# Half of the key tiles of a cross attention turned by VectorE and four transfers a head instead of by TensorE

## The reference

```python
x = layernorm(x + self_attention(x))                 # one head, masked, D = 512
q, k, v = (Q @ Wq + bq), (K @ Wk + bk), (V @ Wv + bv)   # Q = x, K = V = ctx, 16 heads of 64
att = softmax(einsum('bhqd,bhkd->bhqk', q * scale, k))
out = einsum('bhqk,bhkd->bhqd', att, v)
x = layernorm(x + out @ Wo + bo)
x = layernorm(x + shared(x) + expert(x) + bias)
```

## Time and profile before

| | us |
|---|---|
| median of 3 runs | 1958.29 |
| lowest, highest | 1957.91, 1958.37 |
| the profiled execution | 1957.6 |
| its span | 1955.7 |

### The profile page before, as it was taken

How to read it: one execution, slowest core, us unless ns; L and a number is a source line. 1 busy time by engine, 2 the same in 40 slices (tenths; PEclk the granted TensorE clock), 3 DMA queues, 4 the chain that set the end, 5 groups by cost and what they waited for, 6 DMA issues and landing times.

```text
span 1955.7 us, 29661 instructions
## 1 busy us (share of the span) xinstructions
PE 1943.1 (99%) x9863; PEld 1633.1 (84%) x9863; DVE 1475.4 (75%) x3136; ACT 1147.9 (59%) x2461; POOL 727.5 (37%) x858
## 2 busy tenths in 40 slices
PE   9999999999999999999999999999999999999998
PEld 8888888788888888888888888888888888788887
DVE  6766666787777777777777777777777788867887
ACT  5445554676666666666766666666666667732221
POOL 2222342233343433332433333233333343527763
PEclk9999999999999999999999999999999999999999
DMA  5777778863545636354553726355352537321221
GB/s 216 287 282 287 290 280 317 278 223 107 184 167 184 194 108 205 97 184 152 181 170 91 235 74 215 108 161 168 119 186 73 195 121 214 128 87 46 85 87 65
DMA packets 112086, 334.87 MB, mean 171 GB/s; under 512 B 9152, under 2 KB 9152, under 8 KB 107200
## 3 DMA queue, kind: packets, MB, share of 16 engines
q1 hardware_dynamic: 111792, 332.72, 51.0%
q10 hardware_dynamic: 144, 0.26, 0.0%
HBM read 211.31 MB, written 88.08 MB: 153 GB/s over the span
## 4 chain that ended last, share of the span: by engine, by line
PE 95%; DVE 2%; ACT 2%; issue 1%; POOL 0%; ACTq 0%; DVEq 0%; POOLq 0%
PE a_proj L1334 17%; PE a_turned L1334 17%; PE a_score L1347 11%; PE a_av L1371 11%; PE a_proj L48 9%; PE a_proj L1358 5%; PE a_turned L1358 5%; PE a_proj L1762 4%; PE a_av L1762 4%; PE a_score L48 3%; PE a_av L48 3%; ACT c_prob L1042 1%; PE a_score L1737 1%; PE a_turned L1721 1%; PE a_turned L623 1%
## 5 line engine op out<-in xcount | busy, mean ns | idle before, releaser
L981 POOL TENSOR_SCALAR c_prob<-c_prob,all_rden 128x512 f32<-128x512 f32 x512 | 348.6, 693 | 883.5 <-DVE all_rden L1151 883.5
L1042 ACT ACTIVATE c_prob<-a_score,all_negmax 128x512 f32<-128x512 f32 x512 | 347.6, 684 | 212.0 <-DVE all_negmax L1145 209.2
L1145 DVE TENSOR_REDUCE all_negmax<-a_score 128x1 f32<-128x512 f32 x512 | 329.4, 685 | 186.8 <-PE a_score L1347 186.4
L1347 PE MATMUL a_score<-c_ks,c_qs 128*128 128x512 f32 x1024 | 277.6, 391 | 3.2 <-ACT c_prob L1042 2.9
L1371 PE MATMUL a_av<-c_pt,c_vs 128*128 128x512 f32 x1024 | 277.1, 391 | 0.0
L1347 PEld LDWEIGHTS a_score<-c_ks,c_qs 128*128 128x128 f32 x1024 | 190.5, 188 | 44.7 <-ACT c_prob L1042 5.9
L1371 PEld LDWEIGHTS a_av<-c_pt,c_vs 128*128 128x128 f32 x1024 | 192.0, 188 | 39.8
L1191 DVE TENSOR_TENSOR c_pt<-a_proj,c_pt 128x512 fp32r<-128x512 f32 x258 | 171.9, 686 | 26.9 <-ACT c_pt L1070 24.9
L1334 PE MATMUL a_proj<-all_second_buffer,c_wq 128*128 128x512 f32 x756 | 188.0, 397 | 0.0
L1334 PE MATMUL a_turned<-all_third_buffer,all_first_buffer 128*128 128x512 f32 x732 | 182.6, 398 | 0.0
L1191 DVE TENSOR_TENSOR c_pt<-a_turned,c_pt 128x512 fp32r<-128x512 f32 x254 | 169.0, 686 | 9.0 <-ACT c_pt L1070 5.3
(11 more groups left out here) (215 smaller groups left out, 3278.0 us busy)
## 6 DMA issues: line engine op xcount, KB each, us to landing
all_first_buffer<-ctxT_scratch SPq DMA_DIRECT2D x64, 512.0 KB, 7.7
c_wk<-wk_scratch SPq DMA_DIRECT2D x64, 512.0 KB, 3.9
c_wq<-wq_scratch SPq DMA_DIRECT2D x64, 512.0 KB, 6.0
all_second_buffer<-x1T_scratch SPq DMA_DIRECT2D x16, 2048.0 KB, 14.7
c_ks<-c_ks SPq DMA_DIRECT2D x128, 256.0 KB, 6.9
ctxT_scratch<-s_csp SPq DMA_DIRECT2D x8, 2048.0 KB, 7.4
c_y<-y_steps_scratch SPq DMA_DIRECT2D x16, 1024.0 KB, 6.3
y_steps_scratch<-c_y SPq DMA_DIRECT2D x15, 1024.0 KB, 10.2
```

Of the source, the lines that this page charges most:

```text
L981: nc.gpsimd.tensor_scalar(prob[:, n % 2, i, :], prob[:, n % 2, i, :], rden[:, n % 2, i:i + 1], 1.0, ALU.mult, ALU.mult).then_inc(p_ready, 1)
L1042: nc.scalar.activation(prob[:, n % 2, i, :], spsum[:, i % 2, :], ACT.Exp, bias=negmax[:, n % 2, i:i + 1], scale=1.0, accum_out=den[:, n % ...
L1145: nc.vector.tensor_reduce(negmax[:, n % 2, i:i + 1], spsum[:, i % 2, :], AX.X, ALU.max, negate=True).then_inc(smax, 1)
L1347: ins = nc.tensor.matmul(spsum[:, i % 2, :], qs[:, j % 2, e, i * P:(i + 1) * P], ks[:, j % 2, e, m, :], start=(m == HI), stop=(m == LO))
```

## The change

**Two key tiles of four leave PE.** For all heads but the first two and the last (`WHOLE`), key tiles 2 and 3 are turned another way (`FLIPPED` = 2), key tiles 0 and 1 as before. One step turns one tile now (`turned_in`).

**The flip.** DVE transposes squares of 32x32 (`flip`): of each query tile the 256 keys of the two key tiles, 128x256 elements from `prob` to `squares_out`. It reads every fourth key, since a square holds the keys j*4+m of one m. The flips of a step's two tiles stand behind the two maxima of the next step.

**The transfers.** SP sends a head's squares to `landing` with four transfers of 128 KB (`send_squares`): each takes 32 partitions with 4 KB and writes 128 partitions with 1 KB. Two steps later ACT rounds the landed tile to its high part (`flip_hi_tile`) and POOL subtracts it for the low part, in place (`flip_lo_tile`). So two low parts of four move from DVE to POOL.

**The query order.** The columns of a turned tile are now in the order a, i, q (quarter of a query tile, tile, place). PE's transposes write their 128 columns in four pieces of 32, and `o_first` and `o_second` put them back in order. `o_first` writes to `osum` itself, which has room for two pairs, and the sum of a head follows two steps later than its last value.

**The order of projections** is changed in `MIDDLE`, `FIRST` and `LAST`. **The bulk loads** (operands of the next group, Wv, Wo) are issued by ACT in pieces, two behind each of the steps 3, 4 and 6 to 11 (`BULK`); x1T is loaded in four pieces. SP's program goes by steps. The feed-forward weights are stored in pieces, two of its buffers lie elsewhere, and the semaphores `passed` are one.

The core of the diff:

```diff
-    NEXT = ["V0+", "K0+", "Q0+", "V1+", "V2+", "K1+", "Q1+"]
-    MIDDLE = ["V3", "K2", "Q2", "O0", "O1", "O2", "K3", "Q3", "O3"] + NEXT
-    FIRST = ["V2", "V3", "K2", "", "Q2", "", "K3", "", "Q3"]
-    NEXT_TO_FIRST = NEXT
-    LAST = ["V3", "K2", "Q2", "", "O0", "", "K3", "", "Q3", "", "O1", "", "O2", "", "O3", ""]
+    NEXT = ["V0+", "K0+", "Q0+", "V1+", "K1+", "V2+"]
+    MIDDLE = ["Q1", "K2", "Q2", "V3", "O0", "O1", "K3", "Q3", "O2", "O3"] + NEXT
+    FIRST = ["V2", "K2", "Q2", "V3", "", "", "K3", "", "Q3", ""] + NEXT
+    LAST = ["Q1", "K2", "Q2", "V3", "", "O0", "K3", "Q3", "", "O1", "", "O2", "", "O3", "", ""]
...
+    WHOLE = (0, 1, HH * GROUPS - 1)
+    FLIPS = {head: n + 1 for n, head in enumerate(h for h in range(HH * GROUPS) if h not in WHOLE)}
+    LANDINGS = {head: sum(h % 2 == head % 2 for h in FLIPS if h <= head) for head in FLIPS}
+
+    def turned_in(g, step):
+
+        n, half = divmod(step, 2)
+        return [(g, T * n + k) for k in ((2 * half, 2 * half + 1) if HH * g + n in WHOLE else (half,))]
+
+    def valued_in(g, step):
+
+        n, half = divmod(step, 2)
+        tiles = [(n - 1, 1)] if half else [(n - 2, 2), (n - 2, 3), (n - 1, 0)]
+        return [x for x in (tile_of(g, *tile) for tile in tiles) if x]
...
     def head_done(g, step):
 
-        if step % 2 == 0:
-            return None
-        n = (step - 3) // 2
-        return (g, n) if n >= 0 else (g - 1, HH - 1) if g else None
+        n = step // 2 - 2
+        return None if step % 2 else (g, n) if n >= 0 else (g - 1, n + HH) if g else None
...
+    def send_squares(g, n):
+        head = HH * g + n
+        sp.wait_ge(flipped, T * FLIPS[head])
+        wait(sp, av_mm, T * (head - 1))
+        for a in range(SQUARES):
+            sp.dma_start(as_f32(landing[:, head % 2, a, :, :]).rearrange("p k n -> p (k n)"),
+                         squares_out[head % 2][a * Q:(a + 1) * Q].rearrange("p m k i q -> p (m k i q)")).then_inc(
+                             landed[head % 2], 16)
...
+    def flip_lo_tile(g, n, k):
+        head = HH * g + n
+        pool.wait_ge(flip_hi, FLIPPED * (FLIPS[head] - 1) + k + 1)
+        whole = landing[:, head % 2, :, k, :]
+        nc.gpsimd.tensor_tensor(whole, as_f32(whole), by_square(as_f32(flip_hi_part[:, k, :])),
+                                ALU.subtract).then_inc(flip_lo, 1)
...
+    BULK = {3: [("v", (0, 1))], 4: [("v", (2, 3))], 10: [("o", (0, 1))], 11: [("o", (2, 3))], 6: [("c", 0), ("c", 1)], 7: [("c", 2), ("c", 3)], 8: [("x", 0), ("x", 1)], 9: [("x", 2), ("x", 3)]}
...
+    def flip_hi_tile(g, n, k):
+        head = HH * g + n
+        act.wait_ge(landed[head % 2], 16 * SQUARES * LANDINGS[head])
+        wait(act, av_mm, T * (head - 1) + TURNED + k + 1)
+        nc.scalar.copy(by_square(flip_hi_part[:, k, :]), as_f32(landing[:, head % 2, :, k, :])).then_inc(flip_hi, 1)
...
+    def out_part(g, n):
+
+        return osum[sides(n % 2)[0], n // 2 % 2, :].rearrange("p (i a q) -> p i a q", i=T, a=SQUARES)
...
+                for operand, k in BULK.get(step, []):
+                    if operand in "cx":
+                        (load_ctx if operand == "c" else load_x)((g + 1) % NB, k)
+                    if operand == "v" and g % NB == NB - 1:
+                        load_half(act, WV, wvparts, g // NB + 1, wv_loaded, k)
+                    if operand == "o" and g % NB == 0:
+                        wait(act, wo_mm, T * g)
+                        load_half(act, WO, woparts, g // NB, wo_loaded, k)
...
+    def flip(g, t):
+        n, i = divmod(t, T)
+        head = HH * g + n
+        dve.wait_ge(p_ready, TILES * g + t + 1)
+        if i == 0:
+            wait(dve, landed[head % 2], 16 * SQUARES * (LANDINGS[head] - 1))
+        nc.vector.transpose(squares_out[head % 2][:, :, :, i, :].rearrange("p m k q -> p k m q"),
+                            prob[:, n % 2, i, TURNED * P:].rearrange("p (k j m) -> p k m j", k=FLIPPED, m=SQUARES)).then_inc(
+                                flipped, 1)
...
+            for tile in tiles:
+                max_tile(*tile)
+            for tile in ahead(g, step - 1):
+                if HH * tile[0] + tile[1] // T in FLIPS:
+                    flip(*tile)
+            if item and item[0] in "KQ":
+                for e in range(2):
+                    proj_lo_part(item, [e])
+                    if tiles:
+                        recip(*tiles[e])
             else:
-                if left:
-                    rest_of_hole(g, step - 1)
-                for tile in tiles:
-                    max_tile(*tile)
-                finish(item)
+                if item:
+                    finish(item)
                 for tile in tiles:
                     recip(*tile)
-                if head:
-                    o_second(*head)
-                pt_lo_tile(g, 2 * step)
-                pt_lo_tile(g, 2 * step + 1)
+            if head:
+                o_second(*head)
+            for tile in turned_in(g, step):
+                pt_lo_tile(*tile)
...
-            ins = nc.tensor.transpose(bank_of(("T", g, t))[:, i * P:(i + 1) * P],
-                                      prob[:, n % 2, i, k * P:(k + 1) * P], ident[:, :])
+                pe.wait_ge(p_ready, TILES * g + t + i + 1)
+            ins = nc.tensor.transpose(squares(bank_of(("T", g, t)))[:, i], prob[:, n % 2, i, k * P:(k + 1) * P],
+                                      ident[:, :])
...
+            for tile in valued_in(g, step):
+                values(*tile)
+            for tile in turned_in(g, step):
+                turn(*tile)
```

More of the change, by code:

```diff
@@ L1162, in proj_lo_part @@
         bias = bks if letter == "K" else bqs
-        for e in range(2):
+        for e in heads:
             rows, other = sides(e)
@@ L1427, in tensor_all @@
         me.after.gate(0, 0)
+        for t in range(TILES - FLIPPED, TILES):
+            values(GROUPS - 1, t)
         for item in EPILOGUE[:2]:
```

385 lines of the change are left out of this document (184 added, 201 removed).

## The result

The changed kernel takes 1884.54 us (median of 4 runs, 1883.14 to 1884.82), the kernel before 1958.15 us beside it (4 runs, 1957.91 to 1958.37). The ratio is 0.9623, 95% interval 0.9606 to 0.9639: 73.6 us less. The forecast was 1854, 30 us too low. The measured time lies inside the range of 1838 to 1925, but above the stretch of 1840 to 1874 that the forecast itself was given. The profiled execution took 1884.64 us, its span is 1882.7 us.

What follows compares the result with a forecast made beforehand. PE's instruction order was taken to bound the kernel between about 360 and 1730 us. Sum: 1957.6 - 109 (transposes) + 5 (late x1 operand) + 0.7 (end) = 1854 us; range 1838 to 1925, forecast stretch 1840 to 1874 at 0.60.

Steps and rivals of the forecast that it cites:

- rival 1: Cross attention: DVE takes over, its work equal to PE's step at 0.75 us a flip; 1874 to 1924 us, chance 0.11.
- rival 3: Landing of squares takes 15 us where queues are full, ACT stands 1 to 2 us; 1897 to 1945 us, chance 0.10.
- the signs of being right: Four transposes in 0.35 us, 5.00 us steps, PE at 100, flips near 0.42 us, no PE waits for landed low parts.
- the price of a transpose: PE, regular cross attention steps: eight transposes at 0.79 us become four at 0.35, 0.44 us less; 109 us in all.
- The step: PE's regular step in the cross attention falls from 5.44 us to 5.00 us.
- The flip: DVE, two a step: 0.42 us each for 128x256 elements, DVE's work 4.37 us a step, 87% of 5.00.
- The 0.68 us in the prediction: DVE's flip if reading every fourth float halved the rate: 0.68 us instead of 0.42, work 4.89 us a step, still hidden.
- rival 4: DVE's flip is three times as dear, 1.26 us, making the kernel slower at 2110 us; chance 0.07.
- The transfers: A head's squares land in 8 us, wanted by ACT after 11.4 us with some 2 us of slack.
- The operands: The next group's x1 operand may be late by 0 to 1.5 us, 15 times; 5 us taken.
- Rival 2: PE's remaining transposes slow from 110 to 188 ns writing four pieces of 32 columns; 82 us back, 1936 us, chance 0.06.
- The ends: First and last group: 12 steps without a projection lose one transpose chain of 0.35 us each, 4.2 us in all.

Runs made afterwards that it cites:

- The dense read: The changed kernel with the flip reading its keys side by side instead of every fourth, computing another attention: 1891.89 us (0.9661).
- other holes: The changed kernel with the last group's six steps without a projection moved to steps 5, 9, 11, 13, 14, 15: 1882.45 us (0.9618).

## Why the prediction was right, and what failed in it

**The range held by luck.** Its part above 1874 us was there for rival 1 (DVE takes over) and rival 3 (squares land late). Neither happened in the middle; the measured 1884.5 us came into it by a loss that no rival describes. Of the signs of being right, one failed: PE has rows that wait for low parts of landed tiles, 6.1 us in 12.

**The bound and the price of a transpose: right.** PE's order is the time in the middle, and four transposes are worth 0.426 us (forecast 0.44), shown by the period of the groups and once more by putting them back. The step is 5.01 us (5.00). Taking the price from starts of neighbouring chains, and not from the mean of 272 ns in the earlier trace rows, made this term. (The sum counts 12 changed steps without a projection. By the lists `FIRST` and `LAST` there are 10, two of them in the head that isn't flipped, so 8; that moves the sum by 0.4 us.)

**The flip: mis-sized, without effect in the middle.** 0.62 us instead of 0.42, and DVE at 91% instead of 87%. The dense read, at 0.42 us, shows that the whole difference is the stride of 16 bytes. The Trainium skill (SBUF — State Buffer, Door 1: The DMA port swizzle) says that each access that crosses to a new line of 16 bytes pays a penalty, and the trace agrees: the read costs 48% more, 622 ns against 419. The 0.68 us in the prediction was its own estimate, from a rate halved. Rival 1 would have needed a flip of about 0.8 us (estimated above from the run with more work on DVE), rival 4 by the forecast's own sum 0.96 us.

**The transfers: too dear.** 2.7 us at the median, 8.7 at most, so rival 3 fell. By the forecast's sum ACT wants them after 11.4 us. The operands cost 0.8 us of PE's waits in the middle, where 5 were allowed, and 3.4 us in all; 2.5 of these are for ctx, after which the prediction didn't ask. Rival 2 fell as well: a chain of four takes 0.36 us with its output in four pieces of 32 columns, against 0.35 in the earlier trace rows. The rule of the Trainium skill (same page and section) that any non-contiguous PSUM pattern slows matmuls doesn't show in this trace, for pieces of 32 columns.

**The ends: the step that failed.** The prediction gave 12 steps without a projection a gain of 0.35 us each, and 30 regular steps beside them 0.44, and asked after DVE, POOL and the score banks in regular steps alone. There a step has 5 us of PE's work over 4.6 us of DVE's. In a step without a projection PE has 1.7 or 2.6 us left (scores 0.91, values 0.46 or 1.37, a chain 0.35), and DVE still has two maxima, two flips, two reciprocals and a low part, 1.29 + 1.15 + 0.22 + 0.65 = 3.3 us, and in some an output sum besides. There PE need not be the bound, less work for it can be worth nothing, and each operation added elsewhere is a candidate for the path. The run with the transposes twice splits the 29 us: taking them out brought 10.3 of the 17.4 us at the ends, about what the 30 regular steps there would give at 0.426 (12.8), and the rest of the change cost 21.8 us there, which the forecast had at nothing. As time of PE, as far as trace and runs tell, the 29 us are:

- About 18 us are waits of PE. Its listed waits grew by some 19 us over the span (exponentials 2.9 to 9.4, low parts 6.1, ctx 2.5, the feed-forward's x2T 0.8 to 2.7, x1 0.9, two more of 1.0 and 0.4), of which 1.4 us fall into the middle. Of the loss at the start, 4 to 5 us come from heads 0 and 1 turned by PE in succession on single buffers; flipping head 1 shows it.
- Up to 7 us are the clock. In six windows of 10 us, all at the ends, the granted clock is 0.83 to 0.95; the sum of (1 - clock) x 10 us is 6.8 us, though not all of it is time in which PE had work. In the kernel before, the profiled execution had a mean clock of 1.00, here 0.996. It falls behind waits of PE (below). This is read from the trace; no run tried it alone.
- The rest, 4 us or more, is not placed. About 0.5 us of it stands ahead of the stage's first tiles: the same V projection starts at 347.30 us, before at 346.76.

The waits of the last group weren't shortened by other holes or by less work on POOL. The shorter flip took 3.8 us from the stretch behind the 13 groups, in one execution. Whether DVE's order alone sets the pace there, or POOL's order behind DVE's reciprocals, stays open.

## What to carry to other kernels

Price an instruction that leaves a saturated engine by the starts of the rows around it, and then check every stage, the first and last rounds above all, whether that engine is still the bound there: the same edit that gained 0.43 us a step in the middle cost 11 us at the ends. Undo the saving and keep the rest (here: do the transposes twice) to see the hidden cost alone, here 22 us. A special case for a few rounds, like two heads turned the old way, needs its own look at the buffers it shares.
